# Short slots with the next head's norm at their start, in a 6-layer transformer kernel

## The reference

```
for i in range(NL):                       # 6 layers, D = 256, 16 heads of 16, DFF = 1024
    xn = _adaln(x, noise_emb, n1_w[i], n1_b[i])        # layer norm, then scale and shift
    q, k, v = split(xn @ qkv_w[i].T); q, k = _rope(q), _rope(k)
    x = x + _attn(q, k, v, src_mask) @ so_w[i].T       # self attention
    xn = _adaln(x, noise_emb, n2_w[i], n2_b[i])
    q = _rope(xn @ cq_w[i].T); k = _rope(context @ ck_w[i].T); v = context @ cv_w[i].T
    x = x + _attn(q, k, v, ctx_mask) @ co_w[i].T       # cross attention
    xn = _adaln(x, noise_emb, n3_w[i], n3_b[i])
    x = x + gelu(xn @ f1_w[i].T + f1_b[i]) @ f2_w[i].T + f2_b[i]
```

## Time and profile before

| | |
|---|---|
| median of 3 runs | 4429.37 us |
| profiled execution, its own time | 4424.56 us |
| its span | 4422.8 us |
| TensorE (PE) busy | 3947.2 us, 89% |
| VectorE (DVE) busy | 2870.0 us, 65% |
| ScalarE (ACT) busy | 2567.4 us, 58% |
| GpSimd (POOL) busy | 819.0 us, 19% |
| mean granted TensorE clock | 0.965 of full speed |

### The profile page before, as it was taken

How to read it: one execution, slowest core, us unless ns; L and a number is a source line. 1 busy time by engine, 2 the same in 40 slices (tenths; PEclk the granted TensorE clock), 3 DMA queues, 4 the chain that set the end, 5 groups by cost and what they waited for, 6 DMA issues and landing times. The chain is left out here.

```text
span 4422.8 us, 68499 instructions
## 1 busy us (share of the span) xinstructions
PE 3947.2 (89%) x20630; PEld 1837.7 (42%) x20630; DVE 2870.0 (65%) x4716; ACT 2567.4 (58%) x4302; POOL 819.0 (19%) x512
## 2 busy tenths in 40 slices
PE   3889999999999989999989999989999999998558
PEld 1233345433345533354533354533344533354446
DVE  6777766677766677766677766667766677762311
ACT  1566665566665556666566666556666667665112
POOL 3221211111211112121112121112121112110044
PEclk8899999999999999999999999999999999999779
DMA  5634332334332335333244333244333245320235
GB/s 157 151 90 111 96 78 59 78 103 111 87 83 62 71 97 117 86 80 73 64 103 117 87 78 76 59 108 107 91 76 81 61 119 123 95 53 19 67 100 111
DMA packets 271626, 396.39 MB, mean 90 GB/s; under 512 B 28360, under 2 KB 218448, under 8 KB 270928
## 3 DMA queue, kind: packets, MB, share of 16 engines
q1 hardware_dynamic: 263952, 382.18, 35.0%
q0 software_dynamic: 7296, 9.51, 1.3%
HBM read 226.63 MB, written 170.67 MB: 90 GB/s over the span
## 5 line engine op out<-in xcount | busy, mean ns | idle before, releaser
L870 ACT ACTIVATE prob<-ps 128x512 f32<-128x512 f32 x3072 | 1764.9, 595 | 1228.2 <-PE ps L794 1215.7
L1037 DVE TENSOR_REDUCE negmax<-ps 128x2 f32<-128x1024 f32 x1536 | 1828.5, 1219 | 366.8 <-PE ps L821 342.6
L794 PE MATMUL ps<-qstack,kstack 114*128 114x512 bf16 x3072 | 1163.6, 391 | 99.9 <-ACT prob L870 50.9
L807 PE MATMUL psv<-prob,v 128*32 128x512 f32 x6144 | 836.3, 617 | 0.0
L794 PEld LDWEIGHTS ps<-qstack,kstack 114*128 114x128 bf16 x3072 | 286.1, 97 | 1197.2 <-ACT prob L870 743.5
L640 POOL TENSOR_TENSOR rot<-ropep 128x512 f32<-128x512 f32 x94 | 120.0, 1277 | 2621.7 <-DVE ropep L1070 2618.1
L821 PE MATMUL ps<-kstack,qstack 49*128 49x512 bf16 x3072 | 495.3, 388 | 106.7 <-DVE negmax L1037 88.4
L769 PE MATMUL side<-anat,wf 128*128 128x256 f32 x1536 | 377.4, 389 | 9.9 <-DVE hT L1079 8.9
L780 PE MATMUL side<-wf,hT 128*128 128x256 f32 x1536 | 347.9, 379 | 2.8 <-DVE x L1086 1.6
L1079 DVE TENSOR_SCALAR hT<-side,f1b 128x256 f32<-128x256 f32 x384 | 167.3, 477 | 271.3 <-PE side L769 271.3
L769 PEld LDWEIGHTS side<-anat,wf 128*128 128x128 f32 x1536 | 284.6, 191 | 66.0 <-DVE hT L1079 30.6
(11 more groups left out here) (169 smaller groups left out, 3748.0 us busy)
## 6 DMA issues: line engine op xcount, KB each, us to landing
bounce<-parts SPq DMA_DIRECT2D x480, 256.0 KB, 2.5
qstack<-bounce SPq DMA_DIRECT2D x384, 192.0 KB, 5.8
kstack<-bounce SPq DMA_DIRECT2D x384, 192.0 KB, 6.4
bounce<-low SPq DMA_DIRECT2D x96, 256.0 KB, 2.1
ctxT<-in_ctxT SPq DMA_DIRECT2D x24, 512.0 KB, 3.9
w<-in_w SPq DMA_DIRECT2D x16, 512.0 KB, 4.8
wself<-in_wself SPq DMA_DIRECT2D x24, 256.0 KB, 4.4
wcross<-in_wcross SPq DMA_DIRECT2D x24, 256.0 KB, 3.7
```

Of the source, the lines that this page charges most:

```text
L794: nc.tensor.matmul(ps2[:, n % RING2, :], kk[0:ROWS, h, kt * P:(kt + 1) * P], q[0:ROWS, h, :], start=True, stop=True).then_inc(s_p2full, 1)
L807: mm = nc.tensor.matmul(psv[32 * i:32 * i + 32, 0, :], v[j % 2][:, kt, (HD + 1) * h:(HD + 1) * h + 32], prob[:, 4 * (u % 2) + i, :], start ...
L870: nc.scalar.activation(prob[:, 4 * (u % 2) + i, :], ps2[:, n % RING2, :], ACT.Exp, scale=HD ** -0.5).then_inc(s_prob, 1)
L1037: nc.vector.tensor_reduce(out_at, ps1[:, 2 * (n % 2):2 * (n % 2) + 2, :], AX, ALU.max, negate=True).then_inc(s_p1free, 1)
```

## The change

The two tables of short slots become one; its norm is `LN_HT` instead of `LN_NEXT`. The two tables of long slots become one too, with `LN_HT`, so that slot 6 gets the norm that slot 5 did for it; slots 7 to 9 stay as they are. In short slots most chunks of the head come one place earlier (`HQ` from 9, 11 to 9, 10; `HK` from 13, 15 to 12, 14), as do `T1` (5 and 7 for 6 and 8), `T2`, and hi(k) and mid(k) (18, 20 for 19, 21; in slot 2 it was 20, 22). `M` is at place 23 in slot 2 too (24 before). And VectorE's rule `both`, which draws the second maximum of a unit ahead of a heavy chunk at an even place, holds in long slots alone.

```diff
 SHORT = {
-    "M": [23, 0], "HV": [1, 3], "T1": [2, 4, 6, 8], "HT": [5, 7], "HQ": [9, 11], "HK": [13, 15],
...
-    "LN_NEXT": dict(stats=[22, 22, 23, 23], aggregate=24, guess=25, newton=26, tiles=[27, 27, 28, 28]),
-}
-SHORT_AFTER_LONG = {
...
+    "M": [23, 0], "HV": [1, 3], "T1": [2, 4, 5, 7], "HT": [6, 8], "HQ": [9, 10], "HK": [12, 14],
+    "T2": [15, 17], "O": [19, 21], "SPLIT": (13, 15, 18, 20),
+    "LN_HT": dict(stats=[0, 0, 1, 1], aggregate=1, guess=2, newton=3, tiles=[3, 3, 4, 4]),
 }
 LONG = {
...
+    "LN_HT": dict(stats=[0, 0, 0, 0], aggregate=1, guess=2, newton=3, tiles=[3, 4, 4, 5]),
...
-LONG_AFTER_LONG = {**LONG, "LN_HT": dict(stats=[0, 0, 0, 0], aggregate=1, guess=2, newton=3, tiles=[3, 4, 4, 5])}
...
         def places_of(k):
 
-            after_long = k < 2 or is_ffn(k - 1) or k == 2
-            return ((SHORT, SHORT_AFTER_LONG), (LONG, LONG_AFTER_LONG))[is_ffn(k)][after_long]
+            return LONG if is_ffn(k) else SHORT
...
-                    both = any(what in ("HQ", "HK", "O", "F1", "F2") for what, c in plan[2 * u])
+                    both = is_ffn(k) and any(what in ("HQ", "HK", "O", "F1", "F2") for what, c in plan[2 * u])
```

More of the change, by code:

```diff
@@ L51 @@
 SHORT = {
-    "M": [23, 0], "HV": [1, 3], "T1": [2, 4, 6, 8], "HT": [5, 7], "HQ": [9, 11], "HK": [13, 15],
-    "T2": [16, 18], "O": [19, 21], "SPLIT": (13, 15, 19, 21),
-    "LN_NEXT": dict(stats=[22, 22, 23, 23], aggregate=24, guess=25, newton=26, tiles=[27, 27, 28, 28]),
-}
-SHORT_AFTER_LONG = {
[L57 to L60, removed]
+    "M": [23, 0], "HV": [1, 3], "T1": [2, 4, 5, 7], "HT": [6, 8], "HQ": [9, 10], "HK": [12, 14],
+    "T2": [15, 17], "O": [19, 21], "SPLIT": (13, 15, 18, 20),
+    "LN_HT": dict(stats=[0, 0, 1, 1], aggregate=1, guess=2, newton=3, tiles=[3, 3, 4, 4]),
 }
@@ L409, in places_of @@
         def places_of(k):
-            after_long = k < 2 or is_ffn(k - 1) or k == 2
-            return ((SHORT, SHORT_AFTER_LONG), (LONG, LONG_AFTER_LONG))[is_ffn(k)][after_long]
+            return LONG if is_ffn(k) else SHORT
         def norm_steps(k):
             steps, places = [], places_of(k)
-            if "LN_HT" in places and k + 1 < 2 * NJ:
+            if k + 1 < 2 * NJ:
                 steps.append((k, "HT", places["LN_HT"]))
@@ L421, in norm_steps @@
                 steps.append((k, "LT", places["LN_LT"]))
-            if "LN_NEXT" in places and "LN_HT" not in places_of(k + 1) and k + 2 < 2 * NJ:
-                steps.append((k + 1, "HT", places["LN_NEXT"]))
             return steps
@@ L998, in stats @@
                         wait_read(dve, place, k, "O", 1)
-                    elif "LN_HT" not in places_of(k):
-                        wait_read(dve, place, k - 1, "O", 1)
                     elif steps[0]:
```

## The result

The changed kernel took 4387.46 us in the median of four runs (4373.72, 4386.03, 4388.89, 4390.35), against 4429.92 us for the kernel before in the same set; the ratio is 0.9898, 95% interval 0.9876 to 0.9919. Run again among the experiments it came to 0.9875 (0.9857 to 0.9894); one execution of that second set took 9853.6 us at a mean granted clock of 0.482 and is left out of what follows. So the change is 42 to 55 us faster. The forecast was 4410 us, 19 us faster: the sign is right, the size less than half.

A forecast was written before the change was run, and what follows sets the result against it. TensorE, 89% busy, was taken as the bound, with short slots ending 14 to 15 us of DMA chain after the last `low`. Terms 16 - 22 - 15 + 2 + 5 - 5 = -19 us gave 4410 us, forecast 4400 to 4420, range 4386 to 4444.

The forecast's parts named there:

- A: Time from a short slot's start to the end of GpSimd's last `low`; foretold +0.7 us in slots 3 to 5.
- C: Time from the end of the last `low` to the next slot's start; taken as 14.4 us, +0.2 in slots 3 to 5.
- Norm at the start: Norm moved from places 22 to 28 to 0 to 4: +0.8 us before the last `low`, 1.2 freed behind it; slot 6 +0.86.
- Maxima apart: Units 5 to 7 of short slots: second maximum behind a chunk's reading costs 1.4 us, bounds 0 and 2.1; exponential waits -0.3.
- mid(k) half a unit earlier: Short slots, place 20: mid(k) starts behind the second exponential, last `low` ends 1.5 us earlier; bounds 0 and -1.5.
- Shift parts at place 16: Short slots: VectorE's shift steps still meet GpSimd, 0.3 us more than now, bounds -1 and +1.25.
- Clock in the middle: Slots 3 to 5: low clock in 7 of 10 instead of two of three, +0.3 us a layer, +2 us.
- Slot 2 and the start of slot 3: Slot 2 gains 3.6 us six times, -22; slot 3 starts at full clock, 2.6 us six times, -15.
- Slots 0 and 1: Their DMA chain also starts sooner as mid(k) comes two places earlier: -5 us for both, bounds 0 and -8.
- Much faster: Rival: shift parts find GpSimd between instructions, unit 9's wait shortens; 4386 us by the wait alone, stated 4380; chance 0.13.
- Slower: Rival: shift parts at place 16 meet `low` and both key sums, low clock in all 24 short slots; 4448 us; chance 0.17.
- no change: Rival: slots 3 to 5 pay upper bounds of norm and maxima, or slot 3 starts at low clock; 4427 us; chance 0.24.

The follow-up runs named there:

- the -12 measured: Changed kernel with slots 0, 1 and 2 of each layer on their old table, so the change in slots 3 to 6 alone: 4424.53 us, ratio 0.9972.
- slots 0 to 2 alone: Kernel before with the new table, norm at places 0 to 4 and apart maxima in slots 0, 1 and 2 only: 4399.82 us, ratio 0.9913.
- the edit that undoes it: Changed kernel with slots 0 and 1 on their old table, second maximum ahead of heavy chunks there: 4377.71 us, ratio 0.9856.
- the second profiled execution: Changed kernel run once more without edit, in the rounds of the experiments: 4376.56, 4378.77 and 4385.67 us, ratio 0.9875.
- Edits that look alone like 37, 27 and 8 us: Changed kernel with maxima drawn ahead (4344.31 us), first shift parts at place 19 (4355.84), old table in slots 0 and 1 (4377.71); all three: 4321.10.

## Why the prediction was right in sign and short in size

The profiled executions of the kernel before (4422.8 us) and after (4372.0), slots of all six layers added up, against the terms of the sum:

| slots | foretold, us | measured, us |
|---|---|---|
| 0 and 1 | -5 | +11.4 |
| 2 | -22 | -41.2 |
| 3 to 5, with both terms of the clock | +3 | -23.7 |
| 6 | +5 | +6.5 |
| all the rest | 0 | -3.9 |
| sum | -19 | -50.9 |

The sign was right through slot 2, which brought nearly twice what it was given. Slots 3 to 5 and slots 0 and 1 came out with the other sign.

**What bounds the kernel.** Right. A slot ends at A plus a chain of DMAs or TensorE's own work, whichever is longer. With mid(k) late TensorE waits 0.4 to 3.9 us at the end of every short slot, and C of slots 3 to 5 is 13.5 to 17.0 us; in the change it does not wait, and C is its own work, 14.49 us (foretold were 14.05 for that and 14.4 for the chain).

**Norm at the start.** Foretold were 0.8 us more in A of a short slot and 1.2 freed in C. Kind for kind it is 0.5 more in A and 0.7 less in C, both with the waits of the changed kernel and without them, so a short slot gets 0.2 us shorter. The 0.86 of slot 6 came as 0.75 (A from 62.1 to 62.8 us).

**Maxima apart.** Foretold 1.4 us a slot. The two waits are in the trace, 0.44 and 0.54 us, and to draw the maxima ahead again gave 1.2 to 1.3 us a slot of the same kind. The wait of about 0.2 us in unit 8 did not come as one for a maximum: TensorE waits 0.93 us for an exponential there. The -0.3 for exponentials was wrong: in slot 4 these waits rose from 0.6 us to 1.5.

**mid(k) half a unit earlier.** Foretold -1.5 us in A. Without it A is 1.6 us longer in slots of the same kind and the kernel is 47 us slower, 2.0 us a slot with the clock that the waits cost.

**Shift parts at place 16.** This is the step that failed. The prediction took "0.3 more than now, bounds -1 ... and +1.25". Measured: the wait of unit 9 goes from 2.09 to 0.56 us in one kind of slot and to 1.65 in the other, -1.5 and -0.4 us. What was overlooked is that VectorE's place 16 and GpSimd's work both move. In the loop the first step now comes just before the query's `low` instead of behind it, one of three steps is held by `low`, and the third meets the key's first sum or not. The kernels with the steps at place 19 settle that this place is the cause: the edit alone is worth 75 us before the change and 27 after it, so the change had taken part of that gain.

**Clock in the middle.** Foretold +2 us on the ground that "with a wait there as long as now" 7 in 10 slots have it. The wait was not as long. In the profiled executions 10 of the 18 slots 3 to 5 have a low stretch in the middle before, 5 of 18 after, none with the steps at place 19. The 10 before are all in slots 4 and 5; no slot 3 had one. 5 times 1.7 is 8 us, against +2. Together with the shift parts (0.85 us less in the mean of the 18 slots instead of 0.3 more, 21 us) this covers 31 of the 35 us between the +23 us foretold for slots 3 to 6 and the -12 measured.

**Slot 2 and the start of slot 3.** Foretold -22 and -15 us; slots 0 to 2 alone gave -39, and their slots 0 and 1 cost 8 of it, so these two terms are -47 against -37. The wait of 4.00 us went as foretold, and slot 3 starts at full clock; what that brings is less than 15 us where place 16 stays as it was, as slots 0 to 2 alone show. The excess is in slot 2, whose A in the last layer fell by 4.5 us (57.23 to 52.74) and not by 3.0. The prediction had 53.0 for it at full clock and 54.2 with low clock in 7 of 10 slots. That is the same failed step: all six slots 2 have a stretch at 0.50 in the middle before, one has it after, and none in the kernel before with the steps at place 19. Place 16 has its part in A too: the edit there alone takes A of that slot from 57.2 to 53.5. How much of the rest comes from the loop's entry, which differs by some us from one pass to the next, stays open.

**Slots 0 and 1.** Foretold -5 us, measured +8 by the edit that undoes it and in the second profiled execution, +11 in the first. The wait for mrow is 5.4 us instead of 7.7, but the waits for maxima grew by 9.5 (15.4 against 5.9) in slot 0, which has no pass 2 that TensorE could do meanwhile.

**The rivals.** "Much faster" named the right mechanism, the middle wait getting short and the clock going with it, and its 4386 us without the clock is nearest to what was measured. It got 0.13. That the number fits so well is luck: it has 1 us in each of 24 slots and nothing for slot 2 beyond the forecast, for the clock or for slots 0 and 1, and these misses cancel. "Slower" needed a wait of over 3.3 us in unit 9, and "no change" a low start of slot 3 or both upper bounds; neither came. The rule on the port pair (the Trainium skill, "SBUF — State Buffer", Who interferes with whom) holds in the trace: each VectorE step that came behind a GpSimd instruction ended within 0.05 us of its end. What failed was the reading of who meets whom. It had to be worked out from both engines' times, and the bound on the low side should have had the same weight as the one on the high side.

## What to carry to other kernels

When a tiny VectorE operation takes 1 or 2 us, look at what GpSimd does in the same moment, and move the small operation to where GpSimd is idle, before any larger reordering. When a whole table is changed, write the old meeting points of the two engines next to the new ones, since a term with bounds of both signs that is repeated 24 times carries the forecast. And look for the chain that ends the stage: half a unit on ScalarE, in front of that chain, decided 47 us.

## What the runs showed that was not expected

- VectorE's last cast and GpSimd's next sum race when `low` ends. By 0.01 us or less (986.66 against 986.66, 1053.04 against 1053.05) a slot becomes 1.0 us shorter or longer, and 2.6 us with the clock. The same instructions in the same order give both kinds in one execution.
- Among slots 3 to 5 of the profiled execution after the change, the granted clock fell to 0.50 in the middle of 5 of the 11 with a wait of 1.65 us in unit 9, and of none of the 7 with a wait of 0.56 us.
- Edits that look alone like 37, 27 and 8 us gave 63 together. The second gains in slots of the longer kind alone, and in the profiled execution of the first only 7 of 18 are left of them.
